# Rows in front of each expert's queue written at the start, and an expert's last tile moved back to end at its last row

## What is computed

```
h      = norm over the features, then norm over an item's 64 tokens, scaled and shifted per item by a small style network
probs  = softmax(h @ router_w);  gates, idx = top_k(probs, 2);  gates /= gates.sum()
hid    = relu(h @ exp_w1[e] + exp_b1[e]);  eout = hid @ exp_w2[e] + exp_b2[e]      (256 -> 1024 -> 256)
out    = x1 + sum over the two chosen experts of gate * eout
```

## Time and profile before

| | us |
|---|---|
| median of 3 runs | 652.43 (650.9 to 656.67) |
| the profiled execution's own time | 652.26 |
| its span, first to last instruction | 650.4 |
| PE busy | 534.3 (82%) |
| DVE busy | 410.8 (63%) |
| ACT busy | 273.6 (42%) |
| POOL busy | 245.6 (38%) |

### The profile page before, as it was taken

The page is one execution under the profiler, slowest core; times in us unless marked ns, Lnnn a source line. Parts: engine busy times, 40 slices in busy tenths (PEclk is TensorE's granted clock), DMA queues, the critical chain, the costliest instruction groups (busy, mean ns, idle before and its releaser), DMA issues.

```text
span 650.4 us, 15978 instructions
## 1 busy us (share of the span) xinstructions
PE 534.3 (82%) x4352; PEld 452.7 (70%) x4353; DVE 410.8 (63%) x1435; ACT 273.6 (42%) x624; POOL 245.6 (38%) x208
## 2 busy tenths in 40 slices
PE   0868877786844304999999999999999999999992
PEld 0655654574644303888888888888888888888772
DVE  3357989887888671656565656556565646565561
ACT  0326766655565401534253433434353434433350
POOL 4001457776768840132222333322332323232221
PEclk9957888869855555999999999999999999999997
DMA  4334564554345363343333333342333333333321
GB/s 140 115 113 171 191 198 155 187 194 140 103 174 160 118 205 97 42 60 41 57 43 54 57 41 58 40 64 40 58 41 57 55 43 57 41 42 41 51 29 21
DMA packets 78672, 58.41 MB, mean 90 GB/s; under 512 B 51428, under 2 KB 71781, under 8 KB 78501
## 3 DMA queue, kind: packets, MB, share of 16 engines
q1 hardware_dynamic: 64262, 39.20, 21.9%
q0 software_dynamic: 13296, 17.83, 16.3%
q10 hardware_dynamic: 1088, 1.07, 0.5%
HBM read 23.18 MB, written 24.55 MB: 73 GB/s over the span
## 4 chain that ended last, share of the span: by engine, by line
PE 59%; DMA 1%; issue 0%; POOL 0%; ACT 0%; SPq 0%; DVE 0%; POOLq 0%; DVEq 0%
PE banks L1205 30%; PE banks L1221 28%; DMA out<-yg,token 1%; DMA rT<-queues 0%; POOL out L1170 0%; ACT yg L1269 0%; SPq L1142 0%; DVE yb L1338 0%; POOLq L1179 0%; DVEq L1338 0%; SPq L1144 0%; POOLq L84 0%
## 5 line engine op out<-in xcount | busy, mean ns | idle before, releaser
L1170 POOL DMA_INDIRECT out<-yg,token x71 | 114.3, 1609 | 290.0 <-ACT yg L1269 180.5
L1205 PE MATMUL banks<-rT,w_high 128*128 128x256 f16 (+1 forms) x1248 | 198.2, 266 | 23.6 <-DMA rT<-queues 23.0
L1205 PE MATMUL banks<-rT,w_low 128*128 128x256 f16 (+1 forms) x624 | 164.0, 265 | 0.0
L1221 PE MATMUL banks<-w_high,hid_high 128*128 x568 | 154.9, 273 | 0.8 <-issue 0.2
L1221 PE MATMUL banks<-w_low,hid_high 128*128 x568 | 154.8, 273 | 0.0
L1221 PE MATMUL banks<-w_high,hid_low 128*128 x568 | 154.8, 273 | 0.0
L1253 ACT ACTIVATE hid<-banks,feat 128x256 f32<-128x256 f32 (+1 forms) x312 | 119.9, 455 | 65.6 <-PE banks L1205 58.3
L1205 PEld LDWEIGHTS banks<-rT,w_high 128*128 x1248 | 115.0, 99 | 43.1 <-issue 25.1
L1269 ACT ACTIVATE yg<-yb,gate 128x256 f32<-128x256 f32 x71 | 32.6, 501 | 186.2 <-DVE yb L1338 186.2
L1307 DVE TENSOR_TENSOR hid_low<-hid,hid_high 128x512 f16<-128x512 f32 (+1 forms) x156 | 100.9, 647 | 5.3
L1305 DVE CAST hid_high<-hid 128x512 f16<-128x512 f32 (+1 forms) x156 | 67.6, 434 | 46.9 <-issue 23.9
(11 more groups left out here) (176 smaller groups left out, 624.1 us busy)
## 6 DMA issues: line engine op xcount, KB each, us to landing
stage<-expert_w SPq DMA_DIRECT2D x32, 512.0 KB
xb<-x SPq DMA_DIRECT2D x8, 512.0 KB
out<-rb SPq DMA_DIRECT2D x8, 512.0 KB, 3.2
queues<-pad_row SPq DMA_DIRECT2D x5, 260.0 KB
out<-yg,token POOLq DMA_INDIRECT x71, 3.8
queues<-pad_row ACTq DMA_DIRECT2D x4, 260.0 KB
wnow<-w_low SPq DMA_DIRECT2D x8, 128.0 KB, 3.2
queues<-h_rows,slot POOLq DMA_INDIRECT x64
```

Of the source, the lines that this page charges most:

```text
L1170: nc.gpsimd.indirect_dma_start(out=out, out_offset=bass.IndirectOffsetOnAxis(ap=token[:, i.par, s:s + 1], axis=0), in_=yg[:, i.par, s, :], ...
L1205: last = nc.tensor.matmul(ps_in(i, c), w[:, at], features(i)[:, v, k, :], start=(n == 0), stop=(n == 3 * DC - 1))
L1221: last = nc.tensor.matmul(ps_out(i.par)[:, s, :], v[:, i.par, c, s * P:(s + 1) * P], w[:, at], start=(n == 0), stop=(n == 3 * FC - 1))
```

## The change

Four things are altered.

- The padding rows now lie in front of an expert's first row instead of behind its last. `queue_start` begins 256 rows (`SLOTS`) later in each queue. The place of the padding no longer depends on the counts, so POOL writes all nine pieces of 260 KB at the start, right behind its constants. `fill_queues`, `counts` and `counts_known` go, and so does SP's early transfer for `IDLE`.
- DVE writes `pad_row` and the first token numbers before it waits for the first matmuls, instead of after the adapter selection.
- `tile_table` gets one more argument: the end of each queue. A tile's row is now the smaller of its old place and the end less the tile's size. How far it was moved back is kept in `tile_skip`.
- In `gates`, the rows of a tile that the tile before already had (row number below `tile_skip`) get a spare token number. One copy becomes three small instructions.

The diff, cut to its core:

```diff
@@ -353,13 +355,6 @@
             start = sum(CUTS[:2 * LOOP_FROM]) + CUTS[2 * LOOP_FROM] * i.par
             return [((i.half - LOOP_FROM) * STAGES + q, q % STAGES, i.half - LOOP_FROM + q // STAGES)
                     for q in range(start, start + CUTS[2 * LOOP_FROM])]
-
-        def fill_queues(eng, first):
-
-            with eng.Fori(first * EXPERTS // 2, (first + 1) * EXPERTS // 2) as e:
-                count = eng.value_load(counts[0:1, bass.ds(e, 1)], min_val=0, max_val=TOKENS)
-                eng.dma_start(queues[bass.ds(e * QUEUE + count, SLOTS)].rearrange("(s p) d -> p s d", p=P),
-                              bcast(pad_row[:].bitcast(U32), 1, [P, SUB, ROW // 2])).then_inc(filled, 16)
 
         with nc.Block() as block:
...
@@ -399,9 +394,6 @@
 
                 sp.wait_ge(cleared_zero, 1)
                 sp.dma_start(spare_rows, zero_out).then_inc(spare_stored, 16)
-                sp.wait_ge(rows_numbered, 2)
-                sp.dma_start(queues[IDLE:IDLE + SLOTS].rearrange("(s p) d -> p s d", p=P),
-                             bcast(pad_row[:].bitcast(U32), 1, [P, SUB, ROW // 2])).then_inc(filled, 16)
 
                 def body(i):
...
@@ -416,12 +408,9 @@
                         sp.dma_start(of(out_rows, s2.g), rb[:, s2.par]).then_inc(x1_stored[s2.par], 16)
 
                 iterations(sp, body, until=GROUPS // 2 - 1)
-                sp.wait_ge(counts_known, 1)
-                fill_queues(sp, 0)
                 for par in range(2):
                     sp.wait_ge(x1_stored[par], GROUPS // 2 * 16)
                 sp.wait_ge(spare_stored, 16)
-                sp.wait_ge(filled, (EXPERTS + 1) * 16)
 
             @block.gpsimd
...
@@ -446,7 +435,7 @@
                 pool.wait_ge(pool_consts, 7)
                 nc.gpsimd.tensor_copy(earlier16[:], earlier).then_inc(pool_consts, 1)
                 iota(expert_no[:], [[1, EXPERTS]]).then_inc(pool_consts, 1)
-                iota(queue_start[:], [[QUEUE, EXPERTS]]).then_inc(pool_consts, 1)
+                iota(queue_start[:], [[QUEUE, EXPERTS]], base=SLOTS).then_inc(pool_consts, 1)
                 nc.gpsimd.memset(chosen_sum[:], 0.0).then_inc(pool_consts, 1)
 
@@ -456,6 +445,13 @@
                 iota(tile_no[:], [[1, TILES]]).then_inc(rows_cleared, 1)
                 iota(tile_until[:], [[SLOTS, TOKENS // SLOTS]], base=SLOTS).then_inc(rows_cleared, 1)
                 nc.gpsimd.memset(zeros[:], 0.0).then_inc(rows_cleared, 1)
+                iota(row_no[:], [[P, SUB]], channel=1).then_inc(rows_cleared, 1)
+                iota(spare_f[:], [[0, 1]], base=TOKENS, channel=1).then_inc(rows_cleared, 1)
+
+                pool.wait_ge(rows_numbered, 2)
+                for e in range(EXPERTS + 1):
+                    nc.gpsimd.dma_start(queues[e * QUEUE:e * QUEUE + SLOTS].rearrange("(s p) d -> p s d", p=P),
+                                        bcast(pad_row[:].bitcast(U32), 1, [P, SUB, ROW // 2])).then_inc(filled, 16)
 
                 def rstd(g, mv, mv_sem, rs, used_sem, ve_sem, rs_sem):
...
@@ -498,6 +494,7 @@
                 scatter(At(GROUPS // 2, -1), SENDS)
                 for par in range(2):
                     pool.wait_ge(scattered[par], GROUPS // 2 * GT * 2 * 16)
+                pool.wait_ge(filled, (EXPERTS + 1) * 16)
 
             @block.tensor
...
@@ -760,6 +755,9 @@
                 V.tensor_scalar(hot_e, idf[0:ADAPTERS], part_no[0:ADAPTERS, 0:1], None, ALU.is_equal).then_inc(hot_ready, 1)
                 link(V.tensor_scalar(sidf, sidf, 0.0, float(SUBJECTS - 1), ALU.max, ALU.min))
                 V.tensor_scalar(hot_s, sidf, part_no[0:SUBJECTS, 0:1], None, ALU.is_equal).then_inc(hot_ready, 1)
+                dve.wait_ge(rows_cleared, 9)
+                V.tensor_copy(token_field(h_rows[:], "p a t o -> p a (t o)"), first_tokens).then_inc(rows_numbered, 1)
+                V.tensor_copy(pad_row[:, ROW_TOKEN:ROW_TOKEN + 2].bitcast(I32), spare_no).then_inc(rows_numbered, 1)
                 dve.wait_ge(net_done, 1)
                 dve.wait_ge(pool_consts, N_POOL)
...
@@ -1012,13 +1007,12 @@
 
                 count, first, offset, half_rows = (per_expert(k) for k in range(4))
                 parts, taken, scanned = three_per_expert(4), three_per_expert(7), three_per_expert(10)
-                q, rest, whole, half = (per_expert(k) for k in (4, 13, 14, 15))
+                q, rest, whole, half, limit = (per_expert(k) for k in (4, 13, 14, 15, 16))
                 big_small = slice(EXPERTS, 3 * EXPERTS)
                 dve.wait_ge(counted, 1)
                 for par in range(2):
                     dve.wait_ge(x1_stored[par], GROUPS // 2 * 16)
                 dve.wait_ge(nT_done, GROUPS * DC)
-                V.tensor_copy(counts[:], banks[0:1, 6, 0:EXPERTS]).then_inc(counts_known, 1)
                 link(V.tensor_copy(count, banks[:, 6, 0:EXPERTS]))
 
...
@@ -1036,13 +1030,14 @@
                 link(V.tensor_tensor(whole, q, taken[:, EXPERTS:2 * EXPERTS], ALU.add))
                 link(V.tensor_tensor(whole, whole, taken[:, 2 * EXPERTS:3 * EXPERTS], ALU.add))
 
-                def tile_table(number, at, tiles, rows, begin):
+                def tile_table(number, at, tiles, rows, begin, last):
 
                     some = slice(at, at + tiles)
                     no = tile_no[:, 0:tiles]
                     row, used, expert = line(0)[:, 0:tiles], line(1)[:, 0:tiles], tile_expert_f[:, some]
+                    skip = tile_skip[:, some]
                     GRID = [P, tiles, EXPERTS]
-                    g = grid(0)[:, 0:tiles, :]
+                    g, h = grid(0)[:, 0:tiles, :], grid(1)[:, 0:tiles, :]
                     end = scanned[:, 0:EXPERTS]
                     link(V.tensor_tensor_scan(end, number, zeros[:, 0:EXPERTS], 0.0, ALU.add, ALU.add))
                     link(V.tensor_tensor(first, end, number, ALU.subtract))
@@ -1051,26 +1046,32 @@
                     link(V.tensor_scalar(expert, row, -1.0, None, ALU.add))
                     V.tensor_copy(tile_expert[:, some], expert[0:1])
                     link(V.scalar_tensor_tensor(offset, first, -float(rows), begin, ALU.mult, ALU.add))
+                    V.tensor_scalar(limit, last, -float(rows), None, ALU.add)
                     link(V.tensor_tensor(g, bcast(expert, 2, GRID), bcast(expert_no[:], 1, GRID), ALU.is_equal))
+                    V.tensor_tensor(h, g, bcast(limit, 1, GRID), ALU.mult)
                     link(V.tensor_tensor(g, g, bcast(offset, 1, GRID), ALU.mult))
+                    V.tensor_reduce(used, h, AX, ALU.add)
                     link(V.tensor_reduce(row, g, AX, ALU.add))
-                    link(V.scalar_tensor_tensor(row, no, float(rows), row, ALU.mult, ALU.add))
+                    link(V.scalar_tensor_tensor(skip, no, float(rows), row, ALU.mult, ALU.add))
+                    link(V.tensor_tensor(row, skip, used, ALU.min))
+                    V.tensor_tensor(skip, skip, row, ALU.subtract)
                     link(V.tensor_scalar(used, no, end[:, EXPERTS - 1:EXPERTS], None, ALU.is_lt))
                     link(V.scalar_tensor_tensor(row, row, -float(IDLE), used, ALU.add, ALU.mult))
                     return V.tensor_scalar(tile_row[:, some], row[0:1], float(IDLE), None, ALU.add)
 
-                link(tile_table(whole, 0, WHOLE, SLOTS, queue_start[:]))
+                link(V.tensor_tensor(count, count, queue_start[:], ALU.add))
+                link(tile_table(whole, 0, WHOLE, SLOTS, queue_start[:], count))
                 link(V.scalar_tensor_tensor(half_rows, whole, float(SLOTS), queue_start[:], ALU.mult, ALU.add))
                 link(V.tensor_tensor(parts[:, big_small], parts[:, big_small], taken[:, big_small], ALU.subtract))
                 link(V.scalar_tensor_tensor(half, big, 2.0, small, ALU.mult, ALU.add))
-                tile_table(half, WHOLE, HALF, P, half_rows)
+                tile_table(half, WHOLE, HALF, P, half_rows, count)
 
 
 def experts(nc, sem, env):
     queues, out, exp_b2 = env["queues"], env["out"], env["exp_b2"]
-    w_high, w_low, feat, ident16, tile_expert, tile_row, tile_expert_f, banks = (
+    w_high, w_low, feat, ident16, tile_expert, tile_row, tile_expert_f, tile_skip, row_no, spare_f, banks = (
         env[n] for n in ("w_high", "w_low", "feat", "ident16", "tile_expert", "tile_row",
-                         "tile_expert_f", "banks"))
+                         "tile_expert_f", "tile_skip", "row_no", "spare_f", "banks"))
 
     with ExitStack() as ctx:
...
@@ -1314,7 +1317,13 @@
 
                     dve.wait_ge(ratio_ready, i.g + 1)
                     wait(dve, added, (i.subs - before) * 16)
-                    V.tensor_copy(token[:, i.par, n], field(i, ROW_TOKEN, U32))
+                    V.tensor_scalar(valid[:, n], row_no[:, n], tile_skip[:, bass.ds(i.g, 1)], None,
+                                    ALU.is_ge).then_inc(token_step, 1)
+                    dve.wait_ge(token_step, i.g * 2 + 1)
```

(5 more changed lines are left out.)

25 lines of the change are left out of this document (12 added, 13 removed).

## The result

| | before | changed |
|---|---|---|
| median | 653.2 us (10 runs, 650.8 to 656.7) | 660.3 us (10 runs, 658.4 to 661.9) |
| profiled execution | 652.26 (span 650.4) | 661.47 (span 659.5) |

The ratio is 1.0102, with a 95% interval of 1.0075 to 1.0129. The change makes the kernel slower by 7 us. Forecast were 653.9 and a range of 649 to 658.

What follows compares the result with a forecast made beforehand. The prediction took PE's matmuls to bound the experts' block, with the change touching only start and hand-over. It summed 652.26 + 2.2 (start) - 0.6 (hand-over) = 653.9 us, range 649.0 to 658.0.

Steps and rivals of the forecast that it cites:

- What bounds the kernel: Experts' block, 386 us, is bound by PE's matmuls, left unchanged; the change touches only the start and the hand-over between blocks.
- Padding arrives at the start: Start: POOL issues nine transfers at 2.5 us each; three pieces precede x's last packet, delaying PE's start by 2.2 us.
- the sign I had named: Start, new profile: PE's first matmul near 19.3 instead of 17.1, still waiting for x.
- the sign against me: Dense block, 20 to 240 us: if paced by a transfer the padding pushes back, the prediction is wrong altogether.
- all the padding goes ahead of x (slower): PE's first wait, at 17.1: all nine pieces precede x, costing 6.8 us, 659.1 in all; chance 0.14.
- Padding leaves the hand-over: Hand-over to the experts' block: the last scatter lands sooner without padding beside it, -0.6 us, bounds 0 and -1.8.
- Drain, unchanged: POOL's last drain before the experts' block stays at 5.3 us, since it begins when no data moves.
- Tables, +2.2 and hidden: DVE's tables before the experts' block take 2.2 us more, ending at 243.1, hidden under POOL's drain; cost 0.
- Late constants, cost 0: Start: the slow engine's tail moves from 26.2 to at most 33.0 us, before PE and DVE need it at 36.6.
- Experts' block, 0: Experts' block: `gates` grow 0.34 us a tile, at most 1, within DVE's 3.09 us idle; cost 0.

Runs made afterwards that it cites:

- e1: Changed kernel, with POOL's nine padding writes held back until the late constants have landed: 651.0 us, 0.9971 of the kernel before.
- e2: Kernel before, with nine extra early POOL writes into a tensor nobody reads and DVE's two writes moved forward: 658.9 us, ratio 1.0076.
- e4: Changed kernel, with three padding transfers at the start and six after the late constants have landed: 654.0 us, 1.0004 of the kernel before.
- e3: Changed kernel, with the nine padding transfers issued at the start by ACT instead of POOL: 653.3 us, 0.9991 of the kernel before.
- e5: Changed kernel, with the nine padding transfers issued by SP right behind its late constants: 653.7 us, 0.9998 of the kernel before.
- e6: e5 with SP instead of POOL waiting at the dense block's end for scatters and padding to land: 651.2 us, 0.9968 of the kernel before.
- e7: e5 with a POOL drain ahead of each round with scatters and before the last eight scatters: 657.5 us, 1.0057 of the kernel before.
- e8: Changed kernel, with the 17-row adapter table loaded as 16 rows and one: 644.8 us, 0.9870 of the kernel before.

## Why the prediction was wrong, step by step

- **What bounds the kernel.** Right. The difference lies before the experts' block. That block came out 1.0 us shorter by PE's matmuls, more than the 0.5 I allowed, but within the spread of the other kernels. (Its "386 us" is wrong: from PE's first expert matmul to the end it took 397.6.)
- **Padding arrives at the start: the step that failed.** I took twice the scatter, 2.5 us for a piece on POOL, and so three pieces in front of x and +2.2. POOL puts one out each 0.76 us, and the nine were issued by 16.5 us. For x the term was about right all the same: 18.61 and 19.62 in two profiles, +1.5 and +2.5. With the rate wrong by three times, that is luck. But I followed only x. Behind x in the slow engine's line stood the small constants, and PE asks for them 1.9 us after x. They came 5.5 and 5.7 late, as much as seven pieces of 0.76 (an estimate, 5.5 / 0.76). The sum had no term for them; e1 and e2 show that this is the cost: 5.6 us in e2. I had looked at PE's next need of late constants, at 36.6, and passed over the eight early ones, since before the change they raised no wait; only the rival names them, in half a sentence. A row without a wait says nothing about its margin. e4 is the check of my own number: with only three pieces early x and the id rows slip by 1.7, and the kernel takes 654.0. The sign I had named, PE's first matmul near 19.3, came true without saying anything of what stood behind x; the sign against me, a transfer behind 20 us that the padding pushes back, is what came, at 20.5 to 24.5.
- **The rival "all the padding goes ahead of x (slower)".** Its time, 659.1, is near the 660.3 that came, but its path isn't what came: x was 1.5 to 2.5 late and not 6.8, a piece took 0.76 and not 0.6, and PE's first matmul was at 18.61, not 24. Only its clause on the small tensors names the place. Part of the match is luck, since some 2 of the 7.2 us between the profiles belong to the stretch that neither padding nor change explains. I gave it 0.14, with "no scatter is issued faster than one in 1.27 us" against it. A scatter's issue is no guide to that of a plain transfer.
- **Padding leaves the hand-over, -0.6.** The mechanism was right and larger: e3 and e5, with the drain of before, have 17.63 and 17.65 from last slot to block instead of 18.82, so -1.2, inside the bounds of 0 and -1.8.
- **Drain, unchanged.** Wrong by +0.74, nine transfers at 0.082. I reasoned by when data moves; this drain goes by the number of transfers. Both together make -0.46, near my -0.6 by luck.
- **Tables, +2.2 and hidden.** From last slot to DVE's last operation it was 10.93 and is 12.62, so +1.7, hidden under the drain by 5.6 us. Right.
- **Late constants, cost 0.** The tail moved to 31.8, and PE needs them at 44.7. Right, my bound was 33.0.
- **Experts' block, 0.** Right; the gates grew by 0.58 a tile rather than 0.34, under DVE's idle time.

## What to carry to other kernels

When transfers are moved into a stretch where a queue is late, list every tensor still behind the last awaited one, with the time at which it is first used, and not only those that raise a wait now. Look for the transfer whose outer size has no divisor near 16: one engine carrying it is a line that everything else joins, and cutting 17 rows into 16 and 1 was worth more here (645.5 against 653.5 us in the same rounds) than any placing of the padding. Time in which an engine is idle at the start is not free if the queues behind it feed the first link of the chain.

## What the runs showed of the hardware

- POOL issues a plain 260 KB transfer of 256 rows in 0.76 us and one of 128 rows in 0.55, against 1.27 for an indirect one of 128 rows.
- POOL's drain at a block's end, behind its wait for the data, costs 0.082 us for each scatter or padding transfer since the last drain, whatever the number of rows, and about 0.05 for each accumulating one. Without that wait it ran beside the landing (e6: 5.28 us behind the last scatter, the data there after 1.7). Drains in the loop took longer than this rule gives (e7: 1.8 to 4.0 us behind the last scatter).
- The same writes at the same time delay a neighbour's small loads by 5.5 us from POOL's queue and by 0.8 us from ACT's; the records show packets of 3.3 and 0.98 KB. Where the small loads' engine isn't late (e8), they aren't delayed.
- The same f32 matmul of 512 columns takes 592 or 1061 ns while the granted clock reads 1.00.
